# Attention and routed experts on one core: w2 split into high and low parts in advance, w1 fetched for each tile

## The chip, the cores and the metric

The kernel runs on one core of a Trainium2 chip. Its engines are TensorE (PE in the rows; PEld are its weight loads), VectorE (DVE), ScalarE (ACT), GpSimd (POOL) and SyncE (SP, which only issues DMAs here). Each has its own instruction stream, and a small q behind an engine's name (DVEq, PEldq) is its sequencer, which handles registers, branches and waits. The metric is the device time of one execution in microseconds, less is better.

## What is computed

Eight sequences of 512 tokens of width 256, all in float32. The reference, cut to what matters:

```python
def attention(x):                      # x: (8, 512, 256), two heads of width 128
    q = silu(x @ wq); k = sigmoid(x @ wk); v = x @ wv
    f = 1 - k                          # decay
    theta = cumsum(sign(f - 0.5)) * pi
    qr, kr = concat(q*cos, q*sin), concat(k*cos, k*sin)
    out = gla_scan(qr, kr, v, log f)   # S = S*exp(g) + k v^T ; o = q S
    out = out * sigmoid(x @ wg1 @ wg2)
    return layernorm(out) * norm_w @ wo

def experts(x):                        # 8 experts, w1: (8, 1024, 256), w2: (8, 256, 1024)
    aff = x @ centroids.T;  e = argmax(aff);  alpha = sigmoid(aff[e])
    h = relu(layernorm_e(x) @ w1[e].T + b1[e])
    y = x + h @ w2[e].T + b2[e]
    return alpha * y + (1 - alpha) * x

x = x + attention(layernorm(x))
x = x + experts(layernorm(x))
```

## The kernel before

**Attention** runs as a software pipeline over the eight sequences (`pipeline`): in step i an engine works on sequence i (a: projections), i-1 (b: the levels of the scan and the output) and i-2 (c: norm, output projection, second norm, affinities to the centroids). In the first step there is only a, so b and c are None. Within a step the order of each engine's instructions is written out by hand in its `step`. The first step ends on VectorE with the making of the masks (a copy to uint8), which the scan of the next step needs.

**Routing** then sorts the 4096 tokens by expert, in tiles of 128 rows that have one expert each. There are 39 tiles, the number that always suffices, and `tile_expert` in SBUF holds each tile's expert.

**The expert tiles** run in `rounds`, four slots in turn, with a loop over all but the first and last rounds. For a tile t: GpSimd gathers its rows from DRAM by an indirect DMA (`gather`), TensorE transposes them (`z_transposes`), ScalarE applies the expert's gain and bias (`gains`), TensorE multiplies by w1 (`up`, 16 matmuls in float32, which show as 32 in the profile), VectorE adds b1 (`bias_h`), ScalarE makes relu and rounds it to the fast matmul type float32r (`relu`: h_high) and VectorE makes what the rounding lost (`low_h`: h_low). `down` is h @ w2 in float32r with 24 matmuls: for each of 8 k, h_low x w2_high, h_high x w2_low and h_high x w2_high. VectorE finishes (`finish`: y and the output, into k_mix) and GpSimd scatters the rows out. TensorE's turn for t is `up(t+1)`, `z_transposes(t+2)`, `down(t)`. VectorE's turn is `low_h(t)`, the first half of `bias_h(t+1)`, `finish(t-1)`, the second half. GpSimd's turn gathers for t+4, once y of t is finished, and scatters t.

**The weights.** w1 (8 MB) is loaded to `w1_sb` at the start by eight DMAs of 1 MB. w2 (8 MB) is loaded to `w2_sb`, over attention's buffers, once the last sequence has left them. For each tile ScalarE copies the expert's w1 to `w1_now` (`copy_w1`, two halves) and makes w2_high by a rounding copy (`high_w2`, two halves), and w2_low = w2 - w2_high is made in halves by VectorE and GpSimd (`low_w2`, line 446). In the profile `w_sb` is w1_sb, and w2_sb and w1_now are parts of `arena`. Each of these functions reads the expert by `value_load`, a load of a register from SBUF.

## Time and profile before

| | us |
|---|---|
| three runs | 723.04, 729.74, 730.32 |
| median | 729.74 |
| span of the profiled execution | 729.2 |
| of it attention, routing and the first tiles, to the second tile's turn | 425.0 |
| the steady expert tiles, 425.0 to 700.7 | 275.7 |
| the end, from the last `up` | 28.5 |

The profile's span is the time from the first to the last instruction of one execution. It is the number that the stages add up to, and it stands within 0.1% of the median of the runs. Durations and gaps are read from the timeline and the groups of instructions. What an engine waited for is inferred from semaphores, so a wait put down to an engine can be another that came last.

### The profile page before, as it was taken

What the parts mean: (1) busy time and instruction counts of PE and PEld (TensorE: products, weight loads), DVE (VectorE), ACT (ScalarE), POOL (GpSimd) and SP (SyncE); (2) the same over time, 40 slices, a digit from 0 to 9 for tenths busy, and PEclk for the clock granted to TensorE, in tenths of its full rate; (3) what the DMA queues carried; (4) which work ended last, traced back from release to release, by engine and by line L of the source; (5) the groups of instructions that cost most, each with busy time, mean ns of one, the idle gap of its engine ahead of it and who ended that gap; (6) DMA issues with size and microseconds to landing.
All of it is one profiled execution on the core that took longest, in us unless ns stands there. A gap on an engine that the chain in (4) does not pass through costs nothing. (4 is left out here: it accounts for less than half of the span.)

```text
span 729.2 us, 14649 instructions
## 1 busy us (share of the span) xinstructions
PE 609.5 (84%) x3946; PEld 509.7 (70%) x3946; DVE 558.6 (77%) x1068; ACT 433.1 (59%) x835; POOL 347.5 (48%) x384
## 2 busy tenths in 40 slices
PE   4789989859898989987561599999999999999972
PEld 2557677646776767667451598888888888888872
DVE  1486989849898988978347288888888888888982
ACT  4445666536565747454420397777777777777750
POOL 6414251611516052430221347676766766766662
PEclk9889999989999999987655599999999999999995
DMA  8900004040040402020295201111211111112110
GB/s 314 366 1 1 1 30 88 30 88 0 29 86 29 88 31 58 30 59 30 47 382 205 59 23 46 57 51 40 63 36 53 52 43 56 50 38 65 46 27 0
DMA packets 22385, 50.98 MB, mean 70 GB/s; under 512 B 2942, under 2 KB 12544, under 8 KB 20161
## 3 DMA queue, kind: packets, MB, share of 16 engines
q1 hardware_dynamic: 16656, 35.47, 16.3%
q0 software_dynamic: 4992, 14.45, 6.8%
q10 hardware_dynamic: 688, 0.52, 0.2%
q8 instruction: 18, 0.29, 0.2%
q14 instruction: 31, 0.25, 0.1%
HBM read 37.83 MB, written 13.52 MB: 70 GB/s over the span
## 5 line engine op out<-in xcount | busy, mean ns | idle before, releaser
L1163 PE MATMUL bank_a<-masks,arena 128*128 128x128 f32 x1248 | 147.5, 277 | 0.0
L1163 PEld LDWEIGHTS bank_a<-masks,arena 128*128 128x128 f32 x1248 | 144.6, 194 | 0.0
L1180 PE MATMUL bank_c<-w_high,h_low 128*128 128x256 f32 x312 | 94.6, 303 | 20.0 <-POOL w_low L446 14.4
L1236 DVE TENSOR_TENSOR arena<-arena 128x256 f32<-128x256 f32 x224 | 92.6, 455 | 23.3 <-PE bank_l L923 14.4
L923 PEld LDWEIGHTS bank_l<-arena,k_mix 128*128 128x128 f32 x448 | 67.4, 201 | 53.5 <-ACT k_mix L683 27.7
L446 POOL TENSOR_TENSOR w_low<-arena,w_high 128x1024 fp32r<-128x1024 f32 x39 | 95.0, 2437 | 8.3 <-ACT w_high L683 7.7
L683 ACT ACTIVATE arena<-w_sb 128x1024 f32 x78 | 81.8, 1050 | 26.0 <-DVE put_idx L1493 22.3
L1527 DVE SCALAR_TENSOR_TENSOR k_mix<-masks,arena 128x256 f32<-128x256 f32 x39 | 89.3, 2289 | 2.8
L923 PE MATMUL bank_l<-arena,k_mix 128*128 128x128 f32 x448 | 74.5, 292 | 19.9 <-ACT k_mix L683 13.0
L1180 PE MATMUL bank_c<-w_low,h_high 128*128 128x256 f32 x312 | 88.1, 282 | 0.0
L1180 PE MATMUL bank_c<-w_high,h_high 128*128 128x256 f32 x312 | 88.0, 282 | 0.0
L935 PE MATMUL bank_a<-arena 128*128 128x512 f32 x160 | 83.8, 624 | 0.0
L683 ACT ACTIVATE k_mix<-arena 128x128 f32<-128x128 f32 x224 | 61.3, 309 | 36.0 <-DVE arena L1236 35.4
L1180 PEld LDWEIGHTS bank_c<-w_high,h_low 128*128 128x128 f32 x312 | 59.8, 192 | 30.6 <-issue 29.4
L683 ACT ACTIVATE w_high<-arena 128x1024 fp32r x78 | 81.1, 1042 | 0.0
L879 ACT ACTIVATE h_high<-arena 128x512 fp32r<-128x512 f32 x78 | 44.8, 622 | 59.9 <-PE bank_c L1180 59.9
L591 POOL TENSOR_TENSOR arena<-arena 128x512 f32<-128x512 f32 (+6 forms) x56 | 26.2, 467 | 103.7 <-DVE arena L1268 100.0
L1505 DVE TENSOR_TENSOR arena<-bank_a,b_col 128x512 f32<-128x512 f32 x78 | 53.4, 685 | 22.3 <-PE bank_a L1163 12.8
L1514 DVE SCALAR_TENSOR_TENSOR h_low<-arena,h_high 128x512 fp32r<-128x512 f32 x78 | 56.4, 765 | 17.6 <-ACT h_high L879 17.6
L644 POOL DMA_INDIRECT arena<-routed_rows,take_now x39 | 53.9, 1381 | 33.0 <-POOL take_now L642 33.0
L655 POOL DMA_INDIRECT out<-k_mix,put_now x39 | 40.1, 1029 | 46.4 <-issue 36.9
L1180 PEld LDWEIGHTS bank_c<-w_low,h_high 128*128 128x128 f32 x312 | 59.9, 192 | 0.0
(144 smaller groups left out, 1132.6 us busy)
## 6 DMA issues: line engine op xcount, KB each, us to landing
routed_rows<-arena SPq DMA_DIRECT2D x8, 1026.0 KB, 8.9
arena<-x SPq DMA_DIRECT2D x16, 512.0 KB, 4.2
w_sb<-w SPq DMA_DIRECT2D x8, 1024.0 KB, 14.6
arena<-w SPq DMA_DIRECT2D x8, 1024.0 KB, 16.9
arena<-b SPq DMA_DIRECT2D x1, 1024.0 KB, 4.7
arena<-routed_rows,take_now POOLq DMA_INDIRECT x39
out<-k_mix,put_now POOLq DMA_INDIRECT x39, 2.5
arena<-wk SPq DMA_DIRECT2D x1, 256.0 KB, 4.1
```

The lines of the kernel that those rows point to most:

```text
L446: eng.tensor_tensor(w2_low[t.par % 2][:, n * w:(n + 1) * w], w2_sb[:, bass.ds(e * (FC * D) + n * w, w)], w2_high[t.par % 2][:, n * w:(n + ...
L644: pool.indirect_dma_start(out=gathered[p], out_offset=None, in_=rows, in_offset=bass.IndirectOffsetOnAxis(ap=take_now[:, p:p + 1], axis=0) ...
L683: return act.activation(dst, src, ACT.Copy)
L879: act.activation(h_high[:, w], h_sb[:, w], ACT.Relu).then_inc(s_hr, 1)
L923: ins = pe.matmul(bank, k_mix[l % 2][:, m * P:(m + 1) * P], level_queries(buf, m, l), start=True, stop=True)
L935: return pe.matmul(bank[:, :], w[:, i * width + h * P:i * width + (h + 1) * P], xn_t[:, i * T:(i + 1) * T], start=(i == 0), stop=(i == DC ...
L1163: m = pe.matmul(bank_a[k // 4][:, k % 4 * P:(k % 4 + 1) * P], w1_now[:, i * F + k * P:i * F + (k + 1) * P], xl_t[t.par % 2][:, i * P:(i + ...
L1180: m = pe.matmul(bank_c[p][:, 0:D], h[:, k * P:(k + 1) * P], w[p][:, k * D:(k + 1) * D], start=(k == 0 and n == 0), stop=(k == FC - 1 and n ...
L1236: dve.tensor_tensor(half, half, factor(decay[b.par], h, l, second), ALU.mult).then_inc(s_up, 1)
L1505: dve.tensor_tensor(h_sb[:, n * 512:(n + 1) * 512].rearrange("p (k t) -> p k t", t=P), bank_a[n][:, :].rearrange("p (k t) -> p k t", t=P), ...
L1514: dve.scalar_tensor_tensor(out=h_low[:, w], in0=h_sb[:, w], scalar=0.0, in1=h_high[:, w], op0=ALU.max, op1=ALU.subtract).then_inc(s_hl, 1)
L1527: dve.scalar_tensor_tensor(out=y_out[p], in0=y_sb, scalar=gathered[p][:, 2 * D:2 * D + 1], in1=gathered[p][:, D:2 * D], op0=ALU.mult, op1= ...
```

## The change

w2 is split once for each expert instead of once for each tile. SyncE streams w2 in 16 parts of 512 KB (half an expert each) into two buffers `part_raw`. For each part ScalarE makes the high part into `w2_high`, which now stays in SBUF for all experts in the place of w1_sb. VectorE makes the low part into one of two buffers, and SyncE stores it to DRAM (`low_rows`). This is done in attention's first step: six parts ahead of the k sigmoid, four after the first v copy, six at the end of the step, in ScalarE's and in VectorE's order. A part's load waits for the low part of two parts earlier. VectorE waits for all stores before it makes the masks. After attention `w2_low` is loaded for all experts from DRAM, where w2_sb was loaded before.

For each tile SyncE fetches the expert's w1 (1 MB) from DRAM into one of four buffers, once `up` of four tiles earlier is done. `down` reads w2_high and w2_low in place, at an address that TensorE computes from a register with the tile's expert. The copies of ScalarE and the products of VectorE and GpSimd per tile are gone.

```diff
-        w1_sb = sb("w1_sb", [P, E * DC * F], F32)
+        w2_high = sb("w2_high", [P, E * FC * D], F32R)
...
+        PART = 1024
+        PARTS = E * FC * D // PART
+        lay0 = Layout(PHASE1_AB, ARENA)
+        part_low = [lay0.take_rounded("part_low0", PART)]
+        part_raw = [lay0.take(PART)]
+        lay0.take(TJ * D)
+        part_raw.append(lay0.take(PART))
+        lay0.take(TJ * D)
+        part_low.append(lay0.take_rounded("part_low1", PART))
...
-        w2_sb = lay3.take(E * FC * D)
-
-        w2_high = [lay3.take_rounded(f"w2_high{i}", FC * D) for i in range(2)]
-        w2_low = [lay3.take_rounded(f"w2_low{i}", FC * D) for i in range(2)]
+        w2_low = lay3.take_rounded("w2_low", E * FC * D)
+        w1_now = [lay3.take(DC * F) for _ in range(SLOTS)]
...
-        def low_w2(eng, t, n):
-
-            e = eng.value_load(expert_of(t), min_val=0, max_val=E - 1)
-            need(eng, s_ye, 1, before(t, 2), 1)
-            need(eng, s_wh, 2, t, n + 1)
-            w = FC * D // 2
-            eng.tensor_tensor(w2_low[t.par % 2][:, n * w:(n + 1) * w], w2_sb[:, bass.ds(e * (FC * D) + n * w, w)],
-                              w2_high[t.par % 2][:, n * w:(n + 1) * w], ALU.subtract).then_inc(s_wl[n], 1)
...
# SyncE
+            def store_low(n):
+
+                sp.wait_ge(s_low, n + 1)
+                sp.dma_start(low_rows[:, n * PART:(n + 1) * PART], part_low[n % 2].bitcast(F32)).then_inc(s_low_out[n % 2], 16)
...
-            for e in range(E):
-                sp.dma_start(w1_sb[:, e * DC * F:(e + 1) * DC * F], w1_t[:, e * DC * F:(e + 1) * DC * F]).then_inc(s_w1, 16)
+            for n in range(PARTS):
+                if n > 1:
+                    sp.wait_ge(s_low, n - 1)
+                sp.dma_start(part_raw[n % 2], w2_t[:, n * PART:(n + 1) * PART]).then_inc(s_raw[n % 2], 16)
+                if n > 0:
+                    store_low(n - 1)
+            store_low(PARTS - 1)
...
+                    for i in range(2):
+                        sp.wait_ge(s_low_out[i], 16 * (PARTS // 2))
                     for e in range(E):
                         w = slice(e * FC * D, (e + 1) * FC * D)
-                        sp.dma_start(w2_sb[:, w], w2_t[:, w]).then_inc(s_w2, 16)
+                        sp.dma_start(w2_low[:, w].bitcast(F32), low_rows[:, w]).then_inc(s_w2, 16)
...
+            def turn(t):
+                p = t.par
+                e = sp.value_load(expert_of(t), min_val=0, max_val=E - 1)
+                need(sp, s_h, 2, before(t, SLOTS), 2)
+                sp.dma_start(w1_now[p], w1_t[:, bass.ds(e * (DC * F), DC * F)]).then_inc(s_w1[p], 16)
+
+            sp.wait_ge(s_idx, 3)
+            rounds(sp, turn)
...
# GpSimd
-            low_w2(pool, Step(0, 0, SLOTS), 1)
-
             def turn(t):
-                if exists(before(t, -1)):
-                    low_w2(pool, before(t, -1), 1)
...
# ScalarE
+                def parts(i, j):
+                    if b is None and a is not None:
+                        for n in range(i, j):
+                            high(n)
+
                 of(a, xn_copy, 0)
                 of(b, mix, 1, 0)
                 of(a, xn_copy, 1)
+                parts(0, 6)
                 of(b, mix, 1, 1)
                 of(a, k_sigmoid, 0)
...
                 of(a, v_copy, 0)
+                parts(6, 10)
                 of(c, xn2_norm)
                 of(a, v_copy, 1)
                 of(a, gate_sigmoid, 0)
                 of(c, xn2_copies)
                 of(a, gate_sigmoid, 1)
+                parts(10, PARTS)
                 of(nxt, x_norm)
...
+            def high(n):
+
+                act.wait_ge(s_raw[n % 2], 16 * (n // 2) + 16)
+                copy(w2_high[:, n * PART:(n + 1) * PART], part_raw[n % 2]).then_inc(s_high, 1)
...
             def turn(t):
                 relu(t)
-                one = before(t, -1) if exists(before(t, -1)) else None
-                two = before(t, -2) if exists(before(t, -2)) else None
-                if one is not None:
-                    high_w2(one, 0)
-                if two is not None:
-                    copy_w1(two, 0)
-                if one is not None:
-                    high_w2(one, 1)
-                if two is not None:
-                    gains(two)
-                    copy_w1(two, 1)
+                if exists(before(t, -2)):
+                    gains(before(t, -2))
...
# TensorE
                 need(pe, s_xl, DC, t, DC)
+                pe.wait_ge(s_w1[t.par], t.half * 16 + 16)
...
-                        m = pe.matmul(bank_a[k // 4][:, k % 4 * P:(k % 4 + 1) * P], w1_now[:, i * F + k * P:i * F + (k + 1) * P],
+                        m = pe.matmul(bank_a[k // 4][:, k % 4 * P:(k % 4 + 1) * P], w1_now[t.par][:, i * F + k * P:i * F + (k + 1) * P],
...
                 p = t.par % 2
+                e = pe.value_load(expert_of(t), min_val=0, max_val=E - 1)
...
-                        need(pe, s_wh, 2, t, k // 4 + 1)
-                        need(pe, s_wl[k // 4], 1, t, 1)
                     for n, (h, w) in enumerate(((h_low, w2_high), (h_high, w2_low), (h_high, w2_high))):
-                        m = pe.matmul(bank_c[p][:, 0:D], h[:, k * P:(k + 1) * P], w[p][:, k * D:(k + 1) * D],
+                        m = pe.matmul(bank_c[p][:, 0:D], h[:, k * P:(k + 1) * P], w[:, bass.ds(e * (FC * D) + k * D, D)],
...
# VectorE
+                parts(0, 6)
                 of(a, decays, 0)
...
+                parts(6, 10)
                 of(nxt, x_stats)
+                parts(10, PARTS)
                 of(b, states)
...
                 if b is None:
 
+                    for i in range(2):
+                        dve.wait_ge(s_low_out[i], 16 * (PARTS // 2))
                     dve.wait_ge(s_mask, 1)
...
+            def low(n):
+
+                dve.wait_ge(s_high, n + 1)
+                if n > 1:
+                    dve.wait_ge(s_low_out[n % 2], 16 * (n // 2))
+                w = slice(n * PART, (n + 1) * PART)
+                dve.tensor_tensor(part_low[n % 2], part_raw[n % 2], w2_high[:, w], ALU.subtract).then_inc(s_low, 1)
...
                     bias_h(one, 1)
-                    low_w2(dve, one, 0)
```

## Rows read from the trace of the kernel before

**Rows 1.** Busy time by stage: us, then each engine, granted clock, DMA share, GB/s

```profile
425.00:700.70 275.70, 257.15 (x2090) 241.31 (x2089) 237.77 (x253) 210.82 (x289) 190.49 (x178) 1.00 0.17 49
```

**Rows 2.** Timeline of TensorE in the expert stage: start us, us, instruction, idle before

```profile
425.03 3.73 PE L1163 MATMUL bank_a<-masks,arena 128*128 128x128 f32 x32
...
431.65 3.73 PE L1163 MATMUL bank_a<-masks,arena 128*128 128x128 f32 x32
...
500.63 3.73 PE L1163 MATMUL bank_a<-masks,arena 128*128 128x128 f32 x32
...
505.00 0.44 PE L1151 MATMUL bank_b<-ident,arena 128*128 128x128 f32 x2 [0.64 <-DMA arena<-routed_rows,take_now]
...
511.98 0.44 PE L1151 MATMUL bank_b<-ident,arena 128*128 128x128 f32 x2
...
700.70 3.73 PE L1163 MATMUL bank_a<-masks,arena 128*128 128x128 f32 x32
```

**Rows 3.** Waits, 430 to 700 us: who waited for whom, total us, times, longest

```profile
PE bank_c L1180 <- POOL w_low L446: 14.4, 31, 0.7
```

**Rows 4.** Groups, 430 to 700 us: busy us, mean ns | idle before

```profile
L1527 DVE SCALAR_TENSOR_TENSOR k_mix<-masks,arena 128x256 f32<-128x256 f32 x36 | 87.8, 2439 | 2.7
...
L446 POOL TENSOR_TENSOR w_low<-arena,w_high 128x1024 fp32r<-128x1024 f32 x35 | 84.2, 2407 | 0.6 <-issue 0.2
...
L683 ACT ACTIVATE arena<-w_sb 128x1024 f32 x71 | 74.5, 1050 | 2.0
...
L446 DVE TENSOR_TENSOR w_low<-arena,w_high 128x1024 fp32r<-128x1024 f32 x36 | 43.5, 1209 | 0.2 <-issue 0.2
```

**Rows 5.** Timeline of VectorE and GpSimd, one expert tile and the end

```profile
504.55 2.41 DVE L1527 SCALAR_TENSOR_TENSOR k_mix<-masks,arena 128x256 f32<-128x256 f32 x1
...
507.13 0.18 POOL L642 COPY take_now<-take_idx 128x1 int32 x1 [0.46 <-DVE k_mix L1527]
...
508.16 1.42 POOL L644 DMA_INDIRECT arena<-routed_rows,take_now  x1 [0.84 <-POOL take_now L642]
...
707.03 0.48 DVE L1527 SCALAR_TENSOR_TENSOR k_mix<-masks,arena 128x256 f32<-128x256 f32 x1
```

**Rows 6.** Timeline of ScalarE, attention's first step

```profile
12.81 1.28 ACT L717 ACT_TABLE_LOAD   x1
...
15.21 0.60 ACT L717 ACTIVATE arena<-bank_a 128x512 f32<-128x512 f32 x1 [1.12 <-PE bank_a L935]
...
23.83 0.60 ACT L683 ACTIVATE arena<-bank_a 128x512 f32<-128x512 f32 x1 [1.13 <-PE bank_a L964]
```

**Rows 7.** Timeline of VectorE, the masks of the first step

```profile
31.46 2.02 DVE L1396 CAST masks<-arena 128x3584 uint8<-128x3584 f32 x1
```

**Rows 8.** DMA issues: timeline of SyncE, w1's landings, median us to landing

```profile
6.82 4.04 SPq L498 DMA_DIRECT2D w_sb<-w  x8
...
DMA to landing us min/median/max: 7.8/14.6/21.7
...
arena<-b SPq DMA_DIRECT2D x1, 1024.0 KB, 4.7
```

**Rows 9.** Busy time by stretch, inside one store of routed rows

```profile
112.00:115.00 3.00, 2.83 (x13) 1.48 (x11) 2.89 (x12) 1.44 (x5) 1.49 (x2) 1.00 1.05 88
```

**Rows 10.** Sequencer operations of TensorE and ScalarE, and a weight load

```profile
L71 PEldq EVENT_SEMAPHORE  x2: 51/51/51, 505.0 to 505.1; - x2
L71 PEldq ALU_OP  x1: 32/32/32, 505.2 to 505.2; - x1
...
505.30 0.19 PEld L1180 LDWEIGHTS bank_c<-w_high,h_low 128*128 128x128 f32 x1
...
L859 ACTq FUSED_REGOPS  x2: 52/102/152, 501.5 to 501.9; - x2
L859 ACTq TENSOR_LOAD <-tile_expert x1: 281/281/281, 501.6 to 501.6; - x1
```

**Rows 11.** Timeline of VectorE, the last tile

```profile
718.22 0.42 DVE L1522 TENSOR_TENSOR masks<-bank_c,arena 128x256 f32<-128x256 f32 x1 [4.08 <-PE bank_c L1180]
```

More of the change, by code:

```diff
@@ L105, in build_program @@
     rows = nc.dram_tensor("routed_rows", (N, RW), F32, kind="Internal").ap()
+    low_rows = nc.dram_tensor("w2_low_parts", (P, E * FC * D), F32, kind="Internal").ap()
     ctx = ExitStack()
@@ L178, in build_program @@
         h_low = lay3.take_rounded("h_low", F)
-        w1_now = lay3.take(DC * F)
         lay2 = Layout(PHASE1_AB, ARENA)
@@ L253, in build_program @@
         s_small = sem("small_loaded")
-        s_w1 = sem("w1_loaded")
-        s_w2 = sem("w2_loaded")
+        s_w1 = [sem(f"w1_loaded{i}") for i in range(SLOTS)]
+        s_raw = [sem(f"w2_part_loaded{i}") for i in range(2)]
+        s_high = sem("w2_part_high_ready")
+        s_low = sem("w2_part_low_ready")
+        s_low_out = [sem(f"w2_part_low_stored{i}") for i in range(2)]
+        s_w2 = sem("w2_low_loaded")
         s_b2 = sem("b2_loaded")
@@ L327, in build_program @@
         s_hb = sem("h_biased")
-        s_now = sem("w1_now_ready")
-        s_wh = sem("w2_high_ready")
-        s_wl = [sem(f"w2_low{i}_ready") for i in range(2)]
         s_hl = sem("h_low_ready")
@@ L855, in gains @@
                                    bias=b_col[:, bass.ds(e * DC + i, 1)], scale=g_col[:, bass.ds(e * DC + i, 1)]).then_inc(s_xl, 1)
-            def copy_w1(t, n):
-                e = act.value_load(expert_of(t), min_val=0, max_val=E - 1)
-                need(act, s_h, 2, before(t, 1), n + 1)
-                w = slice(n * F // 2, (n + 1) * F // 2)
-                src = w1_sb[:, bass.ds(e * (DC * F), DC * F)].rearrange("p (c f) -> p c f", c=DC)
-                copy(w1_now.rearrange("p (c f) -> p c f", c=DC)[:, :, w], src[:, :, w]).then_inc(s_now, 1)
-            def high_w2(t, n):
-                e = act.value_load(expert_of(t), min_val=0, max_val=E - 1)
-                need(act, s_ye, 1, before(t, 2), 1)
-                w = FC * D // 2
-                copy(w2_high[t.par % 2][:, n * w:(n + 1) * w], w2_sb[:, bass.ds(e * (FC * D) + n * w, w)]).then_inc(s_wh, 1)
             def relu(t):
@@ L882, in turn @@
                 relu(t)
-                one = before(t, -1) if exists(before(t, -1)) else None
-                two = before(t, -2) if exists(before(t, -2)) else None
-                if one is not None:
-                    high_w2(one, 0)
-                if two is not None:
-                    copy_w1(two, 0)
-                if one is not None:
-                    high_w2(one, 1)
-                if two is not None:
-                    gains(two)
-                    copy_w1(two, 1)
-            act.wait_ge(s_w1, 16 * E)
-            act.wait_ge(s_w2, 16 * E)
-            act.wait_ge(s_row_out, 16 * NSEQ + 16)
-            t0, t1 = Step(0, 0, SLOTS), Step(0, 1, SLOTS)
-            for n in range(2):
-                copy_w1(t0, n)
-            gains(t0)
-            gains(t1)
-            for n in range(2):
-                high_w2(t0, n)
-            for n in range(2):
-                copy_w1(t1, n)
+                if exists(before(t, -2)):
+                    gains(before(t, -2))
+            act.wait_ge(s_row_out, 16 * NSEQ + 16)
+            gains(Step(0, 0, SLOTS))
+            gains(Step(0, 1, SLOTS))
             rounds(act, turn)
@@ L1160, in up @@
                         need(pe, s_hb, 2, before(t, 1), k // 4 + 1)
-                        need(pe, s_now, 2, t, k // 4 + 1)
                     for i in range(DC):
-                        m = pe.matmul(bank_a[k // 4][:, k % 4 * P:(k % 4 + 1) * P], w1_now[:, i * F + k * P:i * F + (k + 1) * P],
+                        m = pe.matmul(bank_a[k // 4][:, k % 4 * P:(k % 4 + 1) * P], w1_now[t.par][:, i * F + k * P:i * F + (k + 1) * P],
                                       xl_t[t.par % 2][:, i * P:(i + 1) * P], start=(i == 0), stop=(i == DC - 1))
@@ L1203, in _ @@
             start_at_one(dve, [*s_stat.values(), *s_mom.values(), *s_shift.values(), s_f0, s_q, s_up, s_pick, s_state, s_og,
[L1204 removed]
+                               s_x1, s_at0, s_best, s_hb, s_hl, s_yb, s_yo])
             def sums(n, src, js):
@@ L1324, in output, with parts @@
                     of(b, gating, 1)
+                def parts(i, j):
+                    if b is None and a is not None:
+                        for n in range(i, j):
+                            low(n)
                 def level(l):
```

7 lines of the change are left out of this document (2 added, 5 removed).

## Prediction

> **What bounds the kernel now.** I first cut the span into stages and read each engine's busy time in them. The stretch of the 39 expert tiles, 425.0 to 700.7 us, holds 257 of 276 us of TensorE work at full granted clock, and 238 us of VectorE, 211 of ScalarE, 190 of GpSimd work [rows 1]. It is close to TensorE's bound, but not on it. The timeline of TensorE says by how much. An early tile starts its first layer at 425.03 and the next one at 431.65: 6.62 us with no gap. A later one starts at 500.63, waits 0.64 us for gathered rows at 505.00, and is one of 36 periods from 425.03 to 700.70 [rows 2], that is (700.70 - 425.03)/36 = 7.66 us each. So 1.04 us a tile are waits, 37 us in all. The list of waits gives the half of w_low that GpSimd makes as one cause, 14.4 us [rows 3]. The rest is the row gather, held up behind that same product on GpSimd and behind VectorE's final y (k_mix), which lasts 2.44 us beside it and 0.48 us at the end, where GpSimd is quiet [rows 4, 5].
>
> The second place is the start. There w1 streams in behind other work, and the step of the first sequence has nothing to overlap with: ScalarE, VectorE and TensorE hand one projection to the other, and all later steps queue behind it [rows 6, 7]. Whatever is put into that step in program order is paid in full.
>
> **Part 1: the split moved into the first step, costed.** Sixteen parts of 512 KB go through two buffers. For one buffer the round is: low part made, SyncE wakes (0.1), issues the store (0.45), issues the next load and it lands; then ScalarE's high copy and VectorE's subtraction. The copy is as long as the one of w1 now, 1.05, the subtraction as VectorE's half of w_low, 1.21 [rows 4], 2.46 with 0.1 of semaphore each. The load is not in the trace of before at this size. A lone 1 MB load lands in 4.7 us; w1's eight loads of 1 MB land from 7.8 to 21.7 us after their issues, and from the first issue to the last are 3.6 us (4.04 less the last one's own 0.4), so one follows the other every (21.7 + 3.6 - 7.8)/7 = 2.5 us. So 2.2 us is fixed, and 512 KB take 1.25 more: 3.45 [rows 8]. Behind a store of the same size on the same queue it is up to 4.7. A round is 0.55 + 3.45 + 2.46 = 6.46 at least, 7.7 with the store fully in front; I take 7.1, the middle, as the store is issued only 0.45 ahead. A worse bound: inside the 1 MB store of the rows the queue moved 88 GB/s for three microseconds while reading as full [rows 9]; one such pause in each round makes 10.5.
>
> Start: ScalarE is done with its two copies at 12.8 and loads a table until 14.1; w1's first 1 MB landed at 6.82 + 7.8 = 14.6, so 512 KB do near 13.4 [rows 6, 8]. All parts are in order of program on both engines, and the first six stand ahead of the k sigmoid, so k, q, g1, v come after part 5. That block lasts from 15.21 to 24.43 now [rows 6], 9.2 us; with two copies (2.35) it makes 11.55 between the copies of parts 4 and 6 where a round is 7.1: 4.5 us extra. The last copy (part 15) ends at 14.1 + 7 x 7.1 + 1.3 + 1.05 + 4.5 = 70.7. VectorE adds 1.3 (72.0), the store is issued and lands, 0.1 + 3.45 (75.6), and VectorE, which waits for all stores, then makes the masks, 2.02: 77.6. They end at 33.48 now [rows 7]. Cost: 44 us, with 39.5 to 68 by the two bounds (six or seven rounds at -0.64 and +3.4). What is queued behind the waits: on ScalarE the sigmoids, on VectorE decays and q, on SyncE the x load of the third sequence (not needed before 77), and TensorE for all of them. Nothing covers it: in this step no other sequence is in flight. The masks set the end of the step, the x norm of the next sequence (72 to 74) is just ahead of them. Later attention steps keep their instructions, so the 44 us stay. That the eight loads of w1 vanish gives nothing back, no one waited for them; the eight loads of low parts after attention are those of w2 before.
>
> The Trainium skill ("DMA: Bandwidth & Descriptors", section on the anatomy of one DMA) gives a fixed 2.0 us and 436 GB/s, so 3.2 us for 512 KB where I take 3.45 from the rows. By it the seven rounds are 1.8 us shorter, no other result; its figures were taken for GpSimd's path, and these loads are SyncE's.
>
> **Part 2: start of the expert tiles.** The first w1 fetch is issued once the indices stand and needs 4.7 us [rows 8], about what the first gather needs, with three more fetches behind it and four gathers in the same DMA engines. Nothing of before shows them together. I add 1.5 us, half the transfer of one fetch and some; the bounds are 0 and 4, from fully hidden to a gather behind one and a half fetches of 2.5.
>
> **Part 3: the expert tiles.** Removed per tile: ScalarE two w1 and two w2 copies (4 x 1.05), VectorE 1.21, GpSimd 2.41 [rows 4], and GpSimd's product as VectorE's contender. ScalarE and VectorE then have about half a period of work each, GpSimd its two indirect DMAs with the waits ahead of them, some 4.5 us. w1 comes by 1 MB a tile, 2.5 us of DMA in a period of 7, asked for three tiles ahead: hidden. TensorE gains work for its sequencer: one register load of the expert, and 24 matmuls with an address from a register. On ScalarE the load with its register operations and check lasts 0.28 + 0.15 and small change, 0.6 with the gaps [rows 10]. On TensorE's own sequencer I see three operations between the transposes at 505.00 and the weight load at 505.30 [rows 2, 10], 0.10 us each. How long a matmul with a register address takes to dispatch no row shows. Bounds: nothing (hidden under 0.1165 us, the pace (6.62 - 3.73 - 0.1)/24, 0.1 being what the transposes add), and 0.20, a register operation and a dispatch of 0.10 each. I take p = 0.14: of the three matmuls of a k two need an operation (the w2_high address occurs twice), 0.07 on average, and 0.07 for the dispatch.
>
> The loop through the gather: after a tile's first layer starts (D), VectorE finishes the y before at D + 4.4 (now 504.55 + 2.41 - 500.63 = 6.3; 1.9 less), GpSimd issues the gather 1.2 later (507.13 to 508.16, and 0.17) and works up to 1.4, and rows land 2.4 later as now (508.16 + 1.42 to 511.98) [rows 2, 5]: D + 9.5. They are wanted in the next turn. The sequencer stands at that wait; then come value load and waits for h (1.0), the 24 dispatches and 0.25 for the next tile's waits. Two periods are 9.5 + 1.25 + 24p, so T = 5.4 + 12p: 7.05 at 0.14, 6.8 at 0.117, 7.8 at 0.20. There another loop is longer: h_low is ready at D + 2.1 at the earliest (down's end, relu, VectorE's half), and 2.1 + 1.25 + 24p = 8.15. Sum at 7.05: 36 x (7.66 - 7.05) = 22 us gained.
>
> On the dispatch the Trainium skill ("TensorE: Matmul & The Clock Gate", step-by-step section) says that matmuls and weight loads go to the engine without the sequencer's software, and that where software does it a matmul costs 62 ns. No row shows which holds with a register address. With 0.062 in place of my 0.07 the sum is 3 us lower, and at no cost at all it is the third rival below.
>
> **Part 4: the end.** The last first layer starts at 700.70 and VectorE takes up the last down's result at 718.22 [rows 2, 11], 17.5 later; h_low of both tiles is late there, beside GpSimd's product. After: 3.75, and 2.8 for down(37), 1.6 for relu and h_low, 3.4 for the last down (a little over 24 x 0.1165 for a clock that may fall), 0.15 to VectorE: 11.7 instead of 17.5, 5.8 gained.
>
> **Sum**, against the profiled execution (729.2 span, the runs' median being 729.74, so the two agree): 729.2 + 44 + 1.5 - 22 - 5.8 = 746.9. **Forecast 747 us**, 2.4% slower.
>
> **Rivals.** (A, second) Dispatch bound: p = 0.20 or more. TensorE idles between its matmuls, T = 8.15, 36 x 0.49 = 17.6 lost and only 4 won at the end: 729.2 + 44 + 1.5 + 17.6 - 4 = 788. For it: every register operation seen on that sequencer costs 0.1. Against: the sequencer can work ahead during the first layer. It decides from p = 0.18, where T is 7.66. (B) Stores hold the loads: rounds of 10.5, 44 becomes 68: 771. For it the 88 GB/s stretch [rows 9]; against, 512 KB is short of the 1 MB after which the pause was seen. (C) Not slower: TensorE never waits. If rows land by D + 9 and the dispatch is hidden, T = 6.62 as in the early tiles, 36 x 1.04 = 37.4, end 6.3, start 39.6 + 1: 729.2 + 40.6 - 43.7 = 726. It decides from T = 6.65 with rounds of 6.5. For it the one clean period in [rows 2]; against, gather plus value load fill a period almost exactly.
>
> **Chances.** Forecast 0.45 (its own range 738 to 758), A 0.20, B 0.13, C 0.22. The range is 724 to 789: below lies the part of C where the start costs under 38, above the worst of A. About 1% is what this kernel's runs can tell from nothing. Faster by over 1% (under 722) only in a part of C, 0.06; within 1% (to 737) the rest of C and the edge of the forecast, 0.18; slower 0.76.
>
> **What the new profile would show.** Masks ending near 78 us, a pair of ScalarE's parts every 7 us; no ScalarE copies and no GpSimd product after 412; k_mix at 0.5 us; TensorE's first layers 7.0 us apart. A dispatch bound shows as equal gaps between the second-layer matmuls over 0.12 us. I would be wrong on the start if loads land under 3 us or parts hide; on the tiles if p is far from 0.14.

## The result

The change makes the kernel slower: 749.3 us median (748.3 to 752.3, 4 runs) against 730.0 (723.0 to 732.1, 4 runs), a ratio of 1.030, 95% interval 1.024 to 1.036. The forecast was 747. The profiled execution of the changed kernel took 748.25 us, its span is 746.5, against 729.2 before.

**The start.** ScalarE's timeline of the first step (start us, us, instruction, what ended the idle time):

```profile
12.85 1.99 ACT L700 ACTIVATE w_high<-arena 128x1024 fp32r<-128x1024 f32 x2
21.13 1.06 ACT L700 ACTIVATE w_high<-arena 128x1024 fp32r<-128x1024 f32 x1 [6.29 <-DMA arena<-w]
...
31.05 1.06 ACT L700 ACTIVATE w_high<-arena 128x1024 fp32r<-128x1024 f32 x1 [1.44 <-DMA arena<-w]
32.12 1.28 ACT L734 ACT_TABLE_LOAD   x1
33.41 1.09 ACT L734 ACTIVATE arena<-bank_a 128x512 f32<-128x512 f32 x2
...
63.58 1.06 ACT L700 ACTIVATE w_high<-arena 128x1024 fp32r<-128x1024 f32 x1 [2.66 <-DMA arena<-w]
67.20 1.06 ACT L700 ACTIVATE w_high<-arena 128x1024 fp32r<-128x1024 f32 x1 [2.57 <-DMA arena<-w]
71.15 1.06 ACT L700 ACTIVATE w_high<-arena 128x1024 fp32r<-128x1024 f32 x1 [2.89 <-DMA arena<-w]
74.47 1.06 ACT L700 ACTIVATE w_high<-arena 128x1024 fp32r<-128x1024 f32 x1 [2.27 <-DMA arena<-w]
78.41 1.06 ACT L700 ACTIVATE w_high<-arena 128x1024 fp32r<-128x1024 f32 x1 [2.88 <-DMA arena<-w]
```

Eleven of the sixteen high copies waited for a load, up to 6.3 us. The sigmoid of k, 15.21 in [rows 6], is at 33.41, and the table load that had been in the shade of a projection now stands on the path, behind the copies. The parts use two buffers in turn, so a buffer's round is read from every second row: 71.15 - 63.58 = 7.57, 74.47 - 67.20 = 7.27, 78.41 - 71.15 = 7.26. VectorE's timeline has the end of it:

```profile
45.47 4.57 DVE L1410 TENSOR_TENSOR part_low<-arena,w_high 128x1024 fp32r<-128x1024 f32 x2 [3.70 <-ACT w_high L700]
...
79.50 1.23 DVE L1410 TENSOR_TENSOR part_low<-arena,w_high 128x1024 fp32r<-128x1024 f32 x1 [2.71 <-ACT w_high L700]
84.03 2.03 DVE L1400 CAST masks<-arena 128x3584 uint8<-128x3584 f32 x1 [2.03 <-issue]
```

The masks end at 86.06, against 33.48 in [rows 7]: 52.6 us later. The page's DMA issues say what the rounds wait for:

```profile
arena<-w SPq DMA_DIRECT2D x16, 512.0 KB, 4.9
w_low_parts<-part_low SPq DMA_DIRECT2D x16, 512.0 KB, 3.3
```

A load takes 4.9 us from its issue to its landing (median), a store 3.3.

**The expert tiles.** Busy time of the 36 periods, TensorE's timeline of one ordinary and one long period, the group of the final y, and who waited:

```profile
477.97:724.29 246.32, 241.47 (x2090) 237.31 (x2089) 129.31 (x216) 70.72 (x144) 90.99 (x143) 1.00 0.55 197
```

```profile
484.59 3.74 PE L1159 MATMUL bank_a<-masks,arena 128*128 128x128 f32 x32
...
491.30 3.74 PE L1159 MATMUL bank_a<-masks,arena 128*128 128x128 f32 x32
495.73 0.44 PE L1147 MATMUL bank_b<-ident,arena 128*128 128x128 f32 x2 [0.69 <-DMA arena<-routed_rows,take_now]
496.59 0.38 PE L1175 MATMUL bank_c<-w_high,h_low 128*128 x1 [0.42 <-issue]
...
499.43 3.73 PE L1159 MATMUL bank_a<-masks,arena 128*128 128x128 f32 x32
```

```profile
L1539 DVE SCALAR_TENSOR_TENSOR k_mix<-masks,arena 128x256 f32<-128x256 f32 x36 | 17.5, 485 | 2.7
```

```profile
PE bank_c L1175 <- issue: 2.5, 6, 0.5
PE bank_b L1147 <- DMA arena<-routed_rows,take_now: 1.6, 3, 0.7
```

TensorE works 241.5 of 246.3 us, where it was 257.2 of 275.7 in [rows 1]. A period is (724.29 - 477.97)/36 = 6.84 us, was 7.66. Half of the 36 are 6.53 to 6.62, TensorE's own time for a tile. The others run from 6.65 to 8.14, six of them over 7.05, like 491.30 to 499.43, 8.13, where rows come 0.69 us late and another 0.42 us pass, with nothing to wait for, until the second layer starts. The wait for w_low of [rows 3] is gone with its cause, and k_mix is back at 0.485 us a piece from the 2.439 of [rows 4].

**The entry to the tiles and the end.**

```profile
463.87 0.66 PE L1147 MATMUL bank_b<-ident,arena 128*128 128x128 f32 x2 [10.76 <-DMA arena<-routed_rows,take_now]
...
466.34 8.82 PE L1159 MATMUL bank_a<-masks,arena 128*128 128x128 f32 x64
```

```profile
432.77 0.42 DVE L1445 TENSOR_REDUCE arena<-aff 128x32 f32<-128x256 f32 x1 [1.99 <-ACT aff L700]
```

```profile
735.55 0.42 DVE L1534 TENSOR_TENSOR masks<-bank_c,arena 128x256 f32<-128x256 f32 x1 [1.78 <-PE bank_c L1175]
```

The index chain, VectorE's work that turns affinities into tiles, begins at 432.77, and the first first-layer matmul is at 466.34: 33.6 us, where it was 29.0 (383.87 to 412.84). The first layers of tiles 0 and 1 stand together there (x64), and the 36 periods are counted from that of tile 2, 477.97. At the end VectorE takes up the last tile 735.55 - 724.29 = 11.3 us after the last first layer, 17.5 before [rows 2, 11].

The sum in profiled times: 729.2 + 52.6 (masks) - 3.7 (from the masks' end to the index chain 346.7 us, 350.4 before) + 4.6 (entry) - 0.6 (from tile 0's first layer to tile 2's, 11.6 us, 12.2 before) - 29.4 (36 x 0.82) - 6.3 (end, to the span's end) = 746.4.

### The profile page after: what moved, and what is told of

It reads as the page before. It is cut to its first block and busy times, and to the rows that moved or that the text cites. A ratio compares the mean times of both kernels' runs of the same rounds, so it can differ in the third digit from the quotient of the medians.

```text
span 746.5 us, 14312 instructions
## 1 busy us (share of the span) xinstructions
PE 594.3 (80%) x3946; PEld 503.5 (67%) x3947; DVE 463.4 (62%) x1045; ACT 298.3 (40%) x695; POOL 239.5 (32%) x344
## 5 line engine op out<-in xcount | busy, mean ns | idle before, releaser
L1526 DVE SCALAR_TENSOR_TENSOR h_low<-arena,h_high 128x512 fp32r<-128x512 f32 x78 | 50.7, 691 | 86.9 <-ACT h_high L894 84.1
L931 PE MATMUL bank_a<-arena 128*128 128x512 f32 x160 | 85.9, 637 | 16.6 <-ACT arena L734 16.6
L1175 PE MATMUL bank_c<-w_high,h_low 128*128 x312 | 90.6, 290 | 4.9 <-issue 2.5
L1175 PE MATMUL bank_c<-w_high,h_high 128*128 x312 | 86.9, 278 | 0.0
L1175 PE MATMUL bank_c<-w_low,h_high 128*128 x312 | 86.9, 278 | 0.0
L884 ACT ACTIVATE masks<-bank_b,b_col,g_col 128x128 f32<-128x128 f32 x78 | 31.6, 456 | 134.9 <-PE bank_b L1147 134.9
L676 POOL DMA_INDIRECT out<-k_mix,put_now x39 | 45.1, 1156 | 49.5 <-issue 35.7
L1175 PEld LDWEIGHTS bank_c<-w_high,h_high 128*128 128x128 f32 x312 | 58.7, 188 | 0.0
L1241 DVE COPY_PREDICATED arena<-masks,bank_l 128x256 f32<-128x256 uint8 x112 | 51.2, 523 | 0.0
L665 POOL DMA_INDIRECT arena<-routed_rows,take_now x39 | 38.9, 998 | 32.5 <-POOL take_now L663 32.5
L931 PEld LDWEIGHTS bank_a<-arena 128*128 128x128 f32 x160 | 27.8, 207 | 28.0 <-ACT arena L734 17.9
## 6 DMA issues: line engine op xcount, KB each, us to landing
w_low<-w_low_parts SPq DMA_DIRECT2D x8, 1024.0 KB, 16.6
```

The costliest lines, as they stand in the source:

```text
L665: pool.indirect_dma_start(out=gathered[p], out_offset=None, in_=rows, in_offset=bass.IndirectOffsetOnAxis(ap=take_now[:, p:p + 1], axis=0) ...
L676: pool.indirect_dma_start(out=out, out_offset=bass.IndirectOffsetOnAxis(ap=put_now[:, p:p + 1], axis=0), in_=y_out[p], in_offset=None, bou ...
L931: return pe.matmul(bank[:, :], w[:, i * width + h * P:i * width + (h + 1) * P], xn_t[:, i * T:(i + 1) * T], start=(i == 0), stop=(i == DC ...
L1175: m = pe.matmul(bank_c[p][:, 0:D], h[:, k * P:(k + 1) * P], w[:, bass.ds(e * (FC * D) + k * D, D)], start=(k == 0 and n == 0), stop=(k == ...
L1241: dve.copy_predicated(picked(attn_t[b.par], l, odd), mask, scores.rearrange("p m (n h) -> p m n h", h=2 ** l)).then_inc(s_pick, 1)
L1526: dve.scalar_tensor_tensor(out=h_low[:, w], in0=h_sb[:, w], scalar=0.0, in1=h_high[:, w], op0=ALU.max, op1=ALU.subtract).then_inc(s_hl, 1)
```

## The experiments

Three questions: does each part count by itself, what makes a round 7.4 us, and what sets the tiles' period, now that it is near TensorE's own. The last experiments look for the gains without the price.

**1. No split.**

```
-            for n in range(PARTS): ...   # loads, stores
+            for e in range(E):
+                sp.dma_start(w2_high[...].bitcast(F32), w2_t[...]).then_inc(s_high, 16)
```

> The changed kernel without the split: the raw w2 is loaded whole into w2_high in the first step (eight loads of 1 MB, where w1's stood before) and once more into w2_low after attention; no copy of parts, no subtraction, no store. The products of the second layer are therefore of the wrong parts; their number and timing are as in the changed kernel. Theory (the start costs 52.6 us, the expert tiles and the end give 29.4 + 6.3, each on its own): masks end near 33.5 us, first-layer starts 6.84 us apart, 694 us (692 to 697), a ratio of 0.951 to the kernel before. Rival (a part of the 52.6 us would have been lost in attention anyway, or the tiles gain less without it): over 700 us.

Measured: 700.5 us (694.3 to 703.7), ratio 0.954 (0.949 to 0.959). Masks end at 33.56, the period is 6.83. The gain of the tiles is there whole without the split, and the split is the loss: the medians are 48.8 us apart, close to the 52.6 of the masks. The forecast of 694 was too low, and the time is in the range of the rival, over 700: the profiled run (span 701.7) is 8 us over the sum, 6.2 of it in the entry, 35.2 us from the index chain to the first layer, for which the forecast had taken the 29.0 of before. So the rival's number came true, not its reasons. See 9.

**2. The load issued before the store.**

```
                 sp.dma_start(part_raw[n % 2], ...)
-                if n > 0:
-                    store_low(n - 1)
+                if n > 1:
+                    store_low(n - 2)
```

> The changed kernel, SyncE issues the load of a part before the store of the low part that was just made, instead of behind it. Theory (each round pays the 0.45 us in which the store is issued, and part of the store's transfer in front of the load): seven rounds shorter by 0.45 + half of 1.25, about 7 us less: 741 us, rounds of 6.4 in place of 7.4. Rival (the transfers of both buffers share the DMA engines, so that the order does not matter beyond the issue): 3 us less, 745 us. Rival (the store is in front in full): 12 us less, 736 us.

Measured: 750.1 us, ratio 1.025 (1.023 to 1.027) where the change has 1.030 (1.024 to 1.036); masks at 84.6, 1.5 us sooner. The order matters little: now the stores take 5.6 us where they took 3.3, and the loads still 4.8. The second theory came nearest; "in front in full" is out.

**3. No stores.**

```
-                if n > 0:
-                    store_low(n - 1)
-            store_low(PARTS - 1)
```

> The changed kernel without the sixteen stores of low parts; after attention the raw w2 is loaded in their place (so the low products are wrong, all else is timed as before). Theory (a round is one load of 3.45, two arithmetic instructions and the semaphores, 6.0 us with 0.1 to issue): seven rounds 1.3 us shorter, and 3.4 us for the last store that the masks wait for: 748 - 9 - 3.4 = 736 us. Rival (the loads alone take the 4.9 us that they show, stores or not): 3.4 less, 745 us.

Measured: 739.2 us, ratio 1.010 (1.007 to 1.013); masks at 73.35, 12.7 sooner, of 12.4 expected; of the time 10.2 us less, for 736 expected. ScalarE's rounds and the loads:

```profile
59.61 1.06 ACT L696 ACTIVATE w_high<-arena 128x1024 fp32r<-128x1024 f32 x1 [2.89 <-DMA arena<-w]
61.83 1.06 ACT L696 ACTIVATE w_high<-arena 128x1024 fp32r<-128x1024 f32 x1 [1.16 <-DMA arena<-w]
65.51 1.06 ACT L696 ACTIVATE w_high<-arena 128x1024 fp32r<-128x1024 f32 x1 [2.62 <-DMA arena<-w]
67.83 1.06 ACT L696 ACTIVATE w_high<-arena 128x1024 fp32r<-128x1024 f32 x1 [1.27 <-DMA arena<-w]
```

```profile
arena<-w SPq DMA_DIRECT2D x16, 512.0 KB, 3.6
```

Rounds of 5.9 and 6.0; a load lands in 3.6 us. So beside the stores a load takes 1.3 us longer in the median; the prediction's 7.1 allowed 0.64 for it.

**4. The split late, in place.** w2 is loaded to where its low part will stand, after attention; the split fills idle time of both engines.

```
+            for e in range(E):      # ScalarE, after attention
+                high(e)             # copy(w2_high[e], raw w2[e])
...
+            low(0)                  # VectorE, ahead of its wait for the ranks
+            for e in range(1, E):   # VectorE, behind the indices
+                low(e)              # w2_low[e] = raw w2[e] - w2_high[e]
```

> The changed kernel with the split after attention: the raw w2 is loaded to the place of w2_low as the low parts were; ScalarE makes the high part of each expert as soon as attention is over (8 of 2.1 us, it idles from 431 to 465 us of the changed kernel), VectorE subtracts in place, one expert in its wait for the ranks and seven behind the indices (8 of 2.35 us, it idles from 454.2 to 470.0). No part is stored, nothing is added to the first step. Theory: the start is that of the kernel before, the seven subtractions end 0.5 us after the first layer's result: 694 + 1 = 695 us (693 to 700). Rival (the in-place work beside GpSimd and the row loads runs at the slower rate of 2.28 us a part of 512 KB that two subtractions show at 45.5 us, and the first second-layer product waits for all eight): 36 us of VectorE work where 16 are free, 715 us.

Measured: 702.8 us (701.2 to 709.6), ratio 0.959 (0.957 to 0.961), 4% under the kernel before. It is neither the 695 of the theory nor the 715 of the rival. VectorE's work is as cheap as forecast, and yet the first rows come late. The timelines of VectorE and GpSimd:

```profile
410.48 15.49 DVE L1396 TENSOR_TENSOR w_low<-w_low,w_high 128x2048 fp32r<-128x2048 f32 x7
```

```profile
410.72 2.09 POOL L654 COPY take_now<-take_idx 128x1 int32<-128x1 int32 x1 [6.78 <-DVE put_idx L1492]
413.81 2.26 POOL L656 DMA_INDIRECT arena<-routed_rows,take_now  x1 [1.00 <-POOL take_now L654]
...
426.83 0.97 POOL L656 DMA_INDIRECT arena<-routed_rows,take_now  x1 [0.81 <-POOL take_now L654]
```

Seven subtractions take 15.5 us, 2.2 each. Beside them GpSimd's copy of 128 numbers lasts 2.09 us, without them 0.19, and the gather's issue 2.26, without them 1.24 and less. This is what the rival had in mind, on the other engine: here VectorE is not slowed, GpSimd stands. The first first-layer matmul is 38.0 us behind the start of the index chain. (This profiled run is the slowest of the five, 709.6 us; the stretch ahead of the chain is 4 us longer in it than in the kernel before.)

**5. Three buffers for the parts.**

```
-                if n > 1:
-                    sp.wait_ge(s_low, n - 1)
+                if n > 2:
+                    sp.wait_ge(s_low, n - 2)
```

> The changed kernel with three raw and three low buffers for the parts in place of two; a load is issued as soon as the low part three before is made, ahead of the store of the one before. Loads, stores and arithmetic are the same. Theory (the round is the latency of one load plus arithmetic, now shared by three buffers instead of two: 7.4/3 = 2.5 us a part, where it is 3.7): the start is 16 x 1.2 = 15 to 19 us shorter, 731 us (728 to 735). Rival (bandwidth: 1 MB of load and store per part at the 348 GB/s of the 8 MB load after attention is 3.0 us a part): 9 to 11 us shorter, 739 us. Rival (ScalarE and VectorE in program order, table load and projections between, hold it): under 4 us.

Measured: 739.1 us, where the theory had 731 and the rival with the bandwidth 739; ratio 1.011 (1.008 to 1.015); masks at 72.69, 13.4 sooner. Busy time of 57 to 67 us in this kernel and in the changed one, then ScalarE's copies here:

```profile
57.00:67.00 10.00, 0.00 (x0) 0.00 (x0) 4.73 (x5) 4.22 (x4) 0.00 (x0) 0.59 1.00 391
```

```profile
57.00:67.00 10.00, 5.46 (x8) 2.47 (x8) 5.02 (x11) 3.23 (x5) 1.28 (x2) 0.67 0.83 272
```

```profile
57.36 1.06 ACT L699 ACTIVATE w_high<-arena 128x1024 fp32r<-128x1024 f32 x1 [1.48 <-DMA arena<-w]
59.85 1.06 ACT L699 ACTIVATE w_high<-arena 128x1024 fp32r<-128x1024 f32 x1 [1.44 <-DMA arena<-w]
62.54 1.06 ACT L699 ACTIVATE w_high<-arena 128x1024 fp32r<-128x1024 f32 x1 [1.63 <-DMA arena<-w]
```

A part goes through every 2.5 to 2.7 us, and the DMA share is 1.00 at 391 GB/s: with a third buffer the engines' transfers bound it, 1 MB of load and store a part. With two it is 0.83 and 272 GB/s. So both are half right: latency ruled with two buffers, bandwidth with three, at a better rate than the 348 GB/s I had taken. That the rival's 739 was met is in part luck, as its 3.0 us a part was not.

**6. w1 fetched once.**

```
-            rounds(sp, turn)
+            for i in range(SLOTS):
+                turn(Step(0, i, SLOTS))
```

> The changed kernel in which w1 is fetched for the first four tiles alone; the later tiles use what lies in their slot (the wrong expert's w1), with the same matmuls. Theory (what is left of waits in the expert tiles, 36 x 0.22 = 8 us and the periods of 8.1, is rows that land 4.9 us after their gather is issued, behind the 1 MB of w1 in the same DMA engines, and 2.4 without it): all periods at 6.5 to 6.6, 8 us less, 740 us. Rival (the waits are GpSimd's loop of gather and scatter itself): 6.84 as before, 748 us.

Measured: 746.6 us, where 740 was expected; ratio 1.022 (1.019 to 1.025). In this profiled run the masks end 3.2 us later (89.3), and the stretch from them to the index chain lasts 351.6 us in place of 346.7; nothing in the edit accounts for either, and they hide the gain in the total. The tiles answer the question:

```profile
486.18:725.28 239.10, 238.41 (x2090) 236.75 (x2089) 129.21 (x216) 70.59 (x144) 91.51 (x143) 1.00 0.19 57
```

239.1/36 = 6.64 a period, none over 7.05, TensorE busy for 238.4 of 239.1. The fetches are what makes rows late, and late rows are what the 0.20 us are.

**7. w2 at a fixed address.**

```
-                e = pe.value_load(expert_of(t), min_val=0, max_val=E - 1)
...
-                ... w[:, bass.ds(e * (FC * D) + k * D, D)],
+                ... w[:, k * D:(k + 1) * D],
```

> The changed kernel with the address of w2's parts fixed to the first expert in the second layer: no register load and no register address on TensorE (the products of the other experts are wrong). Forecast of the prediction (a dispatch of 0.14 us a matmul, 12p + 5.4): the period would fall to what static matmuls give, 0.3 us a tile, 11 us in all. Rival, which the equal gaps of 0.117 us between the matmuls in the changed kernel speak for (the dispatch is hidden): period as it is, 6.84 within 0.05, the same time within 3 us.

Measured, one run: 743.8 us.

```profile
482.01:719.85 237.84, 237.00 (x2091) 236.62 (x2090) 129.18 (x216) 70.60 (x144) 92.73 (x143) 1.00 0.57 204
```

The period is 237.84/36 = 6.61. The prediction's form held, 0.3 expected and 0.23 found, and not the rival that the equal gaps spoke for. Equal gaps between matmuls don't show that the sequencer costs nothing: its time lies ahead of the first of them. Numbers 6 and 7 each take away one of two causes, and either way nearly all of the waits are gone: a late row costs time because the register work follows it, and the register work costs time only behind a late row.

**8. Three registers.**

```
-                e = pe.value_load(...)
+                e = [pe.value_load(...) for _ in range(3)]
...
-                ... w[:, bass.ds(e * (FC * D) + k * D, D)],
+                ... w[:, bass.ds(e[n] * (FC * D) + k * D, D)],
```

> The changed kernel with three register loads of the expert per tile, one for each of the three products of a k, so that each of the 24 matmuls of the second layer has an address of its own to work out, where the two of w2_high share one now (16 register operations a tile become 24, and two more loads of some 0.6 us). Theory (the sequencer works ahead during the first layer, whose 3.7 us it needs for nothing): period 6.84 within 0.1. Rival (the sequencer is near its bound, the second of the prediction): the gaps between second-layer matmuls grow to 0.15 us or more, a period of 7.5, 25 us longer.

Measured, one run: 789.2 us, 41 over the changed kernel's profiled run. Busy time of its 36 periods, and the sequencer's operations in one second layer and its register loads; below them the same of a stretch of the changed kernel:

```profile
484.94:763.79 278.85, 266.89 (x2090) 251.73 (x2089) 129.15 (x216) 70.57 (x144) 85.44 (x143) 1.00 0.48 173
```

```profile
L1175 PEldq FUSED_REGOPS  x24: 46/46/51, 520.5 to 523.7; - x24
...
L1167 PEldq TENSOR_LOAD <-tile_expert x3: 296/296/296, 526.3 to 527.5; - x3
```

```profile
L1175 PEldq FUSED_REGOPS  x4: 46/46/46, 503.3 to 504.1; - x4
...
L1175 PEldq ALU_OP  x4: 32/32/32, 503.5 to 504.2; - x4
```

The period is 278.85/36 = 7.75. Of the 24 operations, one per matmul, each starts 0.124 us after the one before where no semaphore lies between, and the matmuls go at 0.125: this is the bound of rival A in kind, though not at its 0.20. In the changed kernel each k has two operations for its three matmuls, and a k takes the sequencer 0.236 us (its first operations start at 503.65, 503.89 and 504.12): 8 x 0.236 = 1.9 us a tile, 0.079 a matmul. The second theory of the expectation came true in its kind, the first is out. Two more register loads (1.3) and eight more operations (24 x 0.124 - 1.9 = 1.1) put 2.4 us on the sequencer; by the prediction's loop over two periods that is 1.2 a period on top of the 5.4 + 12 x 0.079 = 6.35 that the loop gives for the changed kernel, 7.55, and 7.75 is measured. Of the 41 us the periods hold 32.5; another 5.7 lie between the masks and the index chain, where the edit does nothing.

**9 and 10. w1 behind the rows**, in the changed kernel and in that with the late split.

```
+                if isinstance(t.half, int) and number(t) == 1:
+                    sp.wait_ge(s_rows[1], 16)
...
-            sp.wait_ge(s_idx, 3)
+            sp.wait_ge(s_idx, 1)
```

> The changed kernel with the first four fetches of w1 placed otherwise: the first tile's is issued as soon as the tiles' experts stand, ahead of the indices, the next three only when the rows of the second tile have landed. Theory (the first rows of the changed kernel land 6 us late because four fetches of 1 MB go ahead of them in the same DMA engines): from the first step of the index chain to the first first-layer matmul 29.0 us as before the change, where it is 33.6 now, 4.6 less: 744.5 us. Rival (the delay only moves on to the second tile, whose w1 now comes later): first to second first layer 15 or more in place of 11.6, no gain, 749 us.

> The kernel with the split after attention and, with it, the w1 fetches behind the second tile's rows. Theory: the rows of the first tile land 2.6 us behind GpSimd's issue in place of 6.7, of which VectorE's subtractions, done at 426.0, allow all: 4 us less than the kernel with the late split, 698.5 us, a ratio of 0.953. Rival (VectorE's seven subtractions are next, and the second tile waits longer): as with the late split alone, 702.7 us, 0.9585.

Measured: 744.4 us, ratio 1.019 (1.017 to 1.022), and 696.4 us (693.7 to 698.4), ratio 0.954 (0.952 to 0.956). TensorE's timeline in the first of them:

```profile
462.13 0.66 PE L1149 MATMUL bank_b<-ident,arena 128*128 128x128 f32 x2 [6.30 <-DMA arena<-routed_rows,take_now]
...
464.46 9.39 PE L1161 MATMUL bank_a<-masks,arena 128*128 128x128 f32 x64
```

From the index chain (435.49) to the first layer it is 28.97 us again, to the hundredth what it was before the change; from tile 0's first layer to tile 2's (the expectation's "second") it is 12.2. So the 4.6 us of the entry are w1's fetches ahead of the first rows. With the late split the same edit takes the entry from 38.0 to 34.2.

**11. The register loaded early.**

```
             def turn(t):
+                e = pe.value_load(expert_of(t), min_val=0, max_val=E - 1)
                 if exists(before(t, -1)):
                     up(before(t, -1))
...
-                down(t)
+                down(t, e)
```

> The kernel before this one with one more edit: TensorE loads a tile's expert into its register at the start of the turn, ahead of the wait for the next rows, not behind it. Theory (row landing, then register load of 0.64 us, then the addresses, are one loop over two periods; the load moved to where the sequencer is ahead takes 0.3 us a tile from it, down to TensorE's own 6.6): the period falls from 6.84 to 6.6, 8 us less, 690.5 us, a ratio of 0.943. Rival (only the register addresses matter, since with w1's fetches removed the same waits vanished too): no change, 698.5 us.

Measured: 691.0 us (688.9 to 692.7), ratio 0.946 (0.944 to 0.949).

```profile
429.14:668.73 239.59, 238.28 (x2090) 237.03 (x2089) 129.10 (x216) 70.54 (x144) 92.16 (x143) 1.00 0.56 208
```

239.6/36 = 6.66 a period, where number 10 has 6.78, and w1 is fetched for every tile: with the register load ahead of the wait, a late row costs next to nothing. It is the fastest kernel of the study, 39 us under the one before the change.

**12. Short subtractions.**

```
-                dve.tensor_tensor(w2_low[2048 elements], ...)
+                for i in range(4):
+                    dve.tensor_tensor(w2_low[512 elements], ...)
```

> The kernel before this one, each subtraction of 2048 elements by VectorE cut into four of 512. Theory (a small GpSimd instruction that meets VectorE's subtraction waits out that one instruction, 2.2 us, and then runs): GpSimd's copies take 0.8 us and less in place of 2.09, its gathers 1.8 or less in place of 2.26; the first rows land 2.5 us earlier, 688.5 us, a ratio of 0.943. Rival (both share the access evenly, or VectorE takes it back at once): copies and gathers as long as before, and 28 instructions in place of 7 make VectorE 1.5 us longer: 691 to 692 us.

Measured: 694.4 us (692.4 to 694.6), ratio 0.950 (0.947 to 0.952). The forecast was 688.5. It is not faster than number 11; whether it is slower is not clear, as the intervals of the two ratios overlap and the 3.4 us are half a per cent. Timelines of GpSimd, VectorE and TensorE:

```profile
402.47 0.49 POOL L656 COPY take_now<-take_idx 128x1 int32<-128x1 int32 x1 [6.78 <-DVE put_idx L1495]
403.95 1.28 POOL L658 DMA_INDIRECT arena<-routed_rows,take_now  x1 [0.99 <-POOL take_now L656]
```

```profile
402.23 16.94 DVE L1399 TENSOR_TENSOR w_low<-w_low,w_high 128x512 fp32r<-128x512 f32 x28
```

```profile
407.82 0.66 PE L1141 MATMUL bank_b<-ident,arena 128*128 128x128 f32 x2 [6.60 <-DMA arena<-routed_rows,take_now]
...
420.18 5.44 PE L1153 MATMUL bank_a<-masks,arena 128*128 128x128 f32 x32 [4.14 <-DVE arena L1509]
```

The mechanism is as forecast: the copy takes 0.49 us, the gather's issue 1.28, and the first transposes start 5.7 us behind the start of the last index instruction, where it was 8.1. The entry is 3.8 us shorter than in number 11, 30.4 for 34.1. But VectorE now works from 402.2 to 419.2, and the second tile's first layer waits 4.1 us for it; from tile 0's first layer to tile 2's it is 17.6 us, 12.0 in number 11. The late rows had hidden VectorE; the gain went into its wait, and the second layer of the first tile needs all subtractions in any case. One period of 9.1 us lies in this profiled run besides.

## Why the prediction was right, and where it was only lucky

The sign, the place of the loss and the mechanisms held; the total, 746.9 against 746.5, is closer than its terms, whose errors cancel: + 8.6 (masks), - 3.7, + 3.1 (entry, with the 1.5 forecast), - 0.6, - 7.4 (tiles), - 0.5 (end).

- **Part 1, +44: +52.6 at the masks.** The mechanism is right, and the term that failed is the sum of the rounds. From the high copy of one odd part to that of the next (parts 1, 3, ... 15) it is 9.8, 7.4, 14.3, 10.3, 8.0, 7.6 and 7.3 us, 64.6 together, where the prediction has seven times 7.1 and 4.5 once, 54.2; the first copies were 1.6 earlier than forecast. Four things are in the 10.4 us. The steady round is 7.4, since beside the stores a load takes 1.3 longer (number 3), not half of that. In the first round the loads take 5.6 and 6.7 us to land. The block between parts 5 and 6 has the table load of 1.28 on the path, which I had put ahead of the parts, and itself lasts 11.1 us (33.41 to 44.49) where it was 9.2; see the clock below. And part 7's subtraction takes 3.36 us in place of 1.23 (in the 4.57 above), beside a product of GpSimd; see below. By an estimate from the Trainium skill's figures, which the prediction set beside its own ("DMA: Bandwidth & Descriptors", section on the anatomy of one DMA), a load would land in 3.2 us; number 3 has 3.6 without stores, 0.15 above the 3.45 from the rows.
- **"The 44 us stay": 3.7 came back** between the masks and the index chain. This stretch does the same work in all fourteen kernels and lasts 346.7 to 354.7 us in their profiled runs, so that 3.7 can't be told from its scatter. That TensorE does a part of the first step's work in the pauses of the split is possible, and stays open.
- **Part 2, +1.5 (0 to 4): +4.6**, outside its bounds. I had let one and a half fetches stand in front of the rows; with the three later ones moved behind the rows, the 4.6 us are gone (number 9).
- **Part 3, -22: -29.4.** The step that failed is p = 0.14, the sequencer's time for a second-layer matmul. It is 0.079 (number 8), which by the prediction's own sign means that it was wrong on the tiles. An operation with its matmul costs 0.12, against the 0.10 of an operation alone in [rows 10], so the dispatch adds about 0.02 and not 0.07. With p = 0.079, 5.4 + 12p = 6.35 is under TensorE's 6.62, and the loop decides only when rows are late. The 0.6 for the register load was right (526.3 to 527.5 from the first of three to the last in number 8), and its place in the loop too (numbers 7 and 11). That w1's 2.5 us of DMA are hidden was wrong: they cost 0.2 a tile (number 6), as long as the register load stands behind the rows. The Trainium skill ("TensorE: Matmul & The Clock Gate", step-by-step section) says that matmuls can pass without the sequencer's software, and gives 62 ns for one that does not; with a register address the runs agree with the first, since a matmul with its weight load adds 0.02 us to its operation.
- **Part 4, -5.8: -6.3.**
- **Rival A** did not come, but its mechanism is real and near: number 8 builds it with two more loads and eight more operations a tile, and takes 789 us. That this is rival A's 788 is chance: its period is 7.75, not 8.15. **Rival B**, pauses of the stores, is out: rounds are 7.4 us, not 10.5. **Rival C** had the tiles nearly right (6.84, and 6.62 possible) and the start wrong.

Two things of the first step are in no term of the prediction. The first is TensorE's clock. The engine had stood for 16.6 us when the block between parts 5 and 6 reached it at 34.06; in the kernel before it worked without a pause up to the same matmuls. The block's first matmuls in the changed kernel, then in the kernel before:

```profile
34.06:38.00 3.94, 3.94 (x5) 1.85 (x6) 0.69 (x1) 1.07 (x3) 0.00 (x0) 0.50 0.94 366
```

```profile
15.21:19.00 3.79, 3.79 (x10) 1.64 (x9) 0.69 (x1) 2.06 (x4) 2.43 (x11) 1.00 1.02 426
```

The granted clock is 0.50, the lower level of 1.2 GHz, where it was 1.00. Six matmuls of the projection start 0.85 us apart, where they are 0.43 apart at 1.00: 2.5 us, enough for the 1.9 by which the block is longer. The second is GpSimd beside VectorE's subtractions:

```profile
45.65 3.31 POOL L624 TENSOR_TENSOR arena<-arena 128x1024 f32<-128x1024 f32 x1
```

VectorE's first subtraction of the pair is under way when this product starts, and the product takes 3.31 us where the one just before it took 2.36. VectorE's second subtraction starts at 46.69 and takes 3.36.

## What to carry to other kernels

Work that is taken out of a loop has to land where an engine idles: the same split costs 49 us in the first step, where nothing else is in flight, and 2 us after attention, where two engines wait (numbers 1 and 4). When a bulk load is moved next to a small one that someone waits for, issue the small one first; four fetches of 1 MB around the first gather cost 4.6 us once, and one in each tile costs 0.2 us a tile on average. A register load belongs ahead of the wait, where the sequencer has time, not behind it: that was 0.12 us a tile (number 11).

## What the runs showed of the hardware beyond that

- On TensorE's sequencer a register operation with its matmul takes 0.12 us, about the 0.117 us from one such matmul (256 columns) to the next. One new address per matmul is at the limit; two for three (0.236 us for three) are hidden as long as the rows are on time (6.64 us a period in number 6, 6.61 without any in number 7).
- A GpSimd instruction beside VectorE's subtraction of two tiles waits out that instruction: 2.09 us in place of 0.19 beside subtractions of 2.2, 0.49 beside subtractions of 0.6, while VectorE loses nothing. Beside a product of GpSimd it is VectorE that waits, as the 3.36 us in place of 1.23 in the first step show. The Trainium skill ("SBUF — State Buffer", section on the two separate sides) calls it an exclusive lock on a shared port pair, held for the whole instruction; the lengths agree.
- A load of 512 KB lands in 3.6 us without stores and 4.9 beside stores of the same size; with three buffers for each all DMA engines are busy at 391 GB/s.
